# Moving the next input's normalisation into the second cross attention, in a two-block decoder kernel on one Trainium2 core

## What is computed

```python
x = x + L0_attn(layernorm(x))        # one head; scores from shell features
x = x + L0_xattn(layernorm(x), ctx)  # 8 heads over 64 context rows
x = x + L0_ffn(layernorm(x))         # one of 8 experts, chosen per batch
x = x + L1_attn(layernorm(x))        # 16 heads, causal
x = x + L1_xattn(layernorm(x), ctx)  # 16 heads over 64 context rows
x = x + L1_ffn(layernorm(x))         # gated, quantised weights and activations

def L0_attn(x):
    q = tanh(x @ W_charge.T + b_charge)
    shell = normalise(x @ W_shell.T + b_shell)
    proj = shell @ omega.T + rff_bias
    phi = outer(powers(q), concat(cos(proj), sin(proj))) @ W_combine.T
    attn = softmax(causal(phi @ phi.T * decay / temp))
    return (attn @ (x @ W_v.T + b_v)) @ W_out.T + b_out
```

## Time and profile before

| | us |
|---|---|
| median of 3 runs | 3010.41 (3004.92 to 3012.23) |
| the profiled execution | 3010.78 |
| its span, first to last instruction | 3008.8 |
| granted TensorE clock, mean | 0.867 |

### The profile page before, as it was taken

One profiled execution on the slowest core, in us unless ns is written; L12 is line 12 of the kernel. 1 busy time (PEld: TensorE's weight loads), 2 busy tenths in 40 slices (PEclk: granted clock), 3 DMA queues, 4 the chain that ended last, 5 costly groups with the idle time before them and its releaser, 6 DMA issues.

```text
span 3008.8 us, 50636 instructions
## 1 busy us (share of the span) xinstructions
PE 2276.8 (76%) x17470; PEld 1830.6 (61%) x17470; DVE 2175.1 (72%) x4246; ACT 1060.2 (35%) x2004; POOL 585.9 (19%) x666
## 2 busy tenths in 40 slices
PE   3667788868776877886877687888677777888875
PEld 3556666657465756664755565666565566666663
DVE  6765788866866578885776667888586666788767
ACT  2312444422432244442242224444224223444324
POOL 2111222212101122221101112222120102222220
PEclk8778899989777889998877789999877878999988
DMA  6001689840001078983000119897100014899600
GB/s 234 1 15 40 137 160 171 154 86 1 1 15 56 15 149 161 170 152 63 1 1 15 56 37 167 166 164 144 31 1 15 1 55 85 161 169 166 113 1 14
DMA packets 658407, 251.39 MB, mean 84 GB/s; under 512 B 613082, under 2 KB 633946, under 8 KB 657370
## 3 DMA queue, kind: packets, MB, share of 16 engines
q1 hardware_dynamic: 653978, 243.79, 41.4%
q10 hardware_dynamic: 4160, 4.19, 0.4%
HBM read 52.87 MB, written 10.49 MB: 21 GB/s over the span
## 4 chain that ended last, share of the span: by engine, by line
issue 38%; PE 23%; DVE 18%; DMA 11%; ACT 5%; POOL 4%; DVEq 1%; ACTq 0%; SPq 0%; POOLq 0%
DMA l_ptb<-l_phb 6%; PE ps L233 5%; PE ps L235 5%; PE ps L234 4%; DMA l_pts<-l_phs 4%; DVE nmax L1385 3%; PE ps L1289 1%; DVE l_k L1440 1%; DVE l_q L1444 1%; DVE l_phb L1391 1%; DVE l_phs L1391 1%; ACT l_q L1351 1%; PE ps L1271 1%; ACT xn L1347 1%; POOL d_pn L990 1%
## 5 line engine op out<-in xcount | busy, mean ns | idle before, releaser
L1385 DVE TENSOR_REDUCE nmax<-ps 128x1 f32<-128x1024 f32 (+7 forms) x512 | 383.3, 750 | 23.0 <-PE ps L1273 20.9
L1494 POOL CAST l_phb<-l_pb 128x1024 f16<-128x1024 f32 (+3 forms) x256 | 241.4, 943 | 654.1 <-ACT l_pb L1336 337.8
L1336 ACT ACTIVATE l_pb<-ps,nmax 128x1024 f32<-128x1024 f32 (+3 forms) x256 | 244.7, 956 | 283.5 <-DVE nmax L1385 282.7
L1271 PE MATMUL ps<-l_k,l_q 128*128 128x512 f32 (+3 forms) x768 | 319.1, 416 | 24.3 <-ACT l_ps L1336 23.9
L1391 DVE TENSOR_TENSOR l_phb<-l_pb,l_phb 128x1024 f16<-128x1024 f32 (+3 forms) x256 | 288.2, 1126 | 15.5 <-POOL l_phb L1494 13.4
L1272 PE MATMUL ps<-l_k,l_q 128*128 128x512 f32 (+3 forms) x768 | 270.1, 363 | 0.0
L1289 PE MATMUL ps<-l_v,l_ptb 128*128 128x64 f16 x4992 | 197.8, 197 | 34.2 <-DMA l_ptb<-l_phb 34.1
L1289 PEld LDWEIGHTS ps<-l_v,l_ptb 128*128 128x128 f16 x4992 | 177.1, 101 | 67.4 <-DMA l_ptb<-l_phb 41.1
L233 PE MATMUL ps<-xTh,l_w 128*128 128x512 f32 x256 | 123.1, 481 | 83.9 <-DVE l_q L1444 50.5
L1494 POOL CAST l_phs<-l_ps 128x128 f16<-128x128 f32 (+3 forms) x256 | 124.2, 485 | 319.1 <-DMA l_pts<-l_phs 169.6
L1271 PEld LDWEIGHTS ps<-l_k,l_q 128*128 128x128 f32 x768 | 156.0, 203 | 44.2 <-ACT l_ps L1336 29.8
(11 more groups left out here) (361 smaller groups left out, 6279.4 us busy)
## 6 DMA issues: line engine op xcount, KB each, us to landing
l_k<-xn SPq DMA_DIRECT2D x128, 256.0 KB, 4.1
l_w<-l_wqk_s SPq DMA_DIRECT2D x32, 512.0 KB, 4.8
l_wv<-l_wv_s SPq DMA_DIRECT2D x16, 512.0 KB, 6.0
xin<-in_x SPq DMA_DIRECT2D x4, 1024.0 KB, 5.5
m_w<-in_m_w SPq DMA_DIRECT2D x8, 512.0 KB, 4.4
m_w<-in_m_w SPq DMA_DIRECT2D x4, 1024.0 KB, 9.2
l_wo<-in_l_wo SPq DMA_DIRECT2D x16, 256.0 KB, 4.5
l_ptb<-l_phb SPq DMA_TRANSPOSE x256, 4.1
```

What stands on the lines that cost most here:

```text
L1271: pe.matmul(s[:, c0:c1], q, L["l_k1"][:, h, c0:c1], start=True, stop=False)
L1336: s.activation(l_numer(k)[:, 0:n], l_banks(k)[:, 0:n], ACT.Exp, bias=nmax[:, k % 4:k % 4 + 1], accum_out=lsum[:, h, k % NT:k % NT + 1]).th ...
L1385: v.tensor_reduce(nmax[:, k % 4:k % 4 + 1], l_banks(k)[:, 0:n], AX.X, ALU.max, negate=True).then_inc(q_["max"], 1)
L1494: g.tensor_copy(l_parts(k)[:, 0:cols], l_numer(k)[:, 0:cols]).then_inc(q_["hi"], 1)
```

## The change

- The first normalisation leaves the chain. `f_v_norm` has seven steps: 0 to 3 take statistics of two tiles each, 4 aggregates them and makes the reciprocal roots, 5 and 6 write four scaled tiles each. In D with a next batch, steps 0 to 4 stand ahead of `soft(0)` and steps 5 and 6 behind `sum_(1)`. They wait for the load of `xin`. The results lie in arrays of their own (`n_*`), in memory that D leaves free and that G's `g_h` and later arrays take over.
- At the head of G, PE transposes the four groups into four banks (4 to 7): two behind `turn_x(0)`, one behind `turn_x(1)`, one behind `updown(1)`. ACT copies two ahead of `silu(0)`, one ahead of and one behind `silu(1)`. DVE's residuals stand two ahead of `hidden(0)` and two behind it.
- All later steps of the chain come two values of t sooner on every engine. The combinations of four tiles and the two last value groups move ahead of `down(6)`, and DVE's second combination ahead of `add(7)`. The combination products use two banks in turn, where they had six.
- `f_pe_value` ends each value tile with one matmul of a row of ones with `bvo`; POOL's addition to `xin` and the wait for it are gone.
- The opening pass runs the same steps, the normalisation in one piece.

Cut to its core:

```diff
+        def f_v_norm(v, b, k, w):
+            if k < 4:
+                if k == 0:
+                    v.wait_ge(s_xin, b * 16 + 16)
+                for t in (2 * k, 2 * k + 1):
+                    v.bn_stats(w["n_st"][:, t, :], xin[:, t, :])
+            elif k == 4:
+                v.drain()
+                for t in range(NT):
+                    v.bn_aggr(w["n_ag"][:, t, :], w["n_st"][:, t, :])
+                v.drain()
+                v.tensor_scalar(w["n_nv"][:], w["n_ag"][:, :, 1], EPS, None, ALU.add)
+                rsqrt(v, w["n_rsd"][:], w["n_nv"][:])
+            else:
+                for t in range(4 * (k - 5), 4 * (k - 5) + 4):
+                    v.tensor_scalar(w["n_xn"][:, t, :], xin[:, t, :], w["n_ag"][:, t, 0:1], w["n_rsd"][:, t:t + 1],
+                                    ALU.subtract, ALU.mult).then_inc(s_x0, 1)
+        def f_pe_turn(pe, b, g, w):
+            pe.wait_ge(s_x0, b * NT + 4 * (g // 2) + 4)
+            for c in range(DC):
+                for t in range(2):
+                    o = ps[:, f_bank(g), c * 256 + t * P:c * 256 + (t + 1) * P]
+                    last = pe.transpose(o, w["n_xn"][:, 2 * g + t, c * P:(c + 1) * P], idf[:])
+            last.then_inc(s_tr, 1)
...
         def f_pe(pe, b, t):
-            if t in (0, 1):
-                ln_pe(pe, b, 0, (2 * t, 2 * t + 1))
-            elif t == 2:
+            if t == 0:
                 pe.wait_ge(s_lo, ln_done(b, 0))
...
+            elif t in (4, 5):
+                for u in (2 * t - 8, 2 * t - 7):
+                    pe.wait_ge(a_sem["ph"], b * 2 + 1)
+                    if u < 2:
+                        pe.wait_ge(a_sem["va"], b * 4 + u + 1)
+                    else:
+                        pe.wait_ge(a_sem["ya"], b * NT + u - 1)
+                    f_pe_comb(pe, u)
             elif t == 6:
                 pe.wait_ge(C0.s["kvT"], b * 2 + 2)
...
+                pe.wait_ge(a_sem["ph"], b * 2 + 2)
+                for u in range(4, NT):
+                    if u < 6:
+                        pe.wait_ge(a_sem["ya"], b * NT + u - 1)
                     f_pe_comb(pe, u)
                 for g in (2, 3):
-                    pe.wait_ge(a_sem["ya"], b * NT + g + 1)
                     f_pe_value(pe, b, g)
+            elif t == 7:
                 x_pe_m(pe, C0, b)
...
         def comb_bank(u):
-            return (0, 1, 2, 3, 6, 7, 0, 1)[u]
+            return (6, 7, 6, 7, 6, 7, 0, 1)[u]
...
                 for c in range(DC):
-                    last = mm3(pe, o, xTh[:, c, tok], xTl[:, c, tok], wvo_h[:, c, :], wvo_l[:, c, :], c == 0, c == DC - 1)
+                    mm3(pe, o, xTh[:, c, tok], xTl[:, c, tok], wvo_h[:, c, :], wvo_l[:, c, :], c == 0, False)
+                last = pe.matmul(o, ones_f[0:1, :], bvo[0:1, :], start=False, stop=True)
             last.then_inc(a_sem["v"], 1)
...
         def f_g(g, b):
             x_diagonal_first(g, b)
-            g.wait_ge(s_xn, b * (NPH * NT) + NT)
-            g.tensor_tensor(xin[:], xin[:], bvo[:].unsqueeze(1).to_broadcast([P, NT, D]), ALU.add).then_inc(s_xb, 1)
...
         def x_v(v, cr, b, more=False):
...
+            if more:
+                for k in range(5):
+                    f_v_norm(v, b + 1, k, N)
             soft(0)
             soft(1)
             sum_(0)
             sum_(1)
+            if more:
+                for k in (5, 6):
+                    f_v_norm(v, b + 1, k, N)
...
             turn_x(0)
+            if more:
+                f_pe_turn(pe, b + 1, 0, N)
+                f_pe_turn(pe, b + 1, 1, N)
             pe.wait_ge(g_sem["xT"], b * 2 + 1)
...
             turn_x(1)
+            if more:
+                f_pe_turn(pe, b + 1, 2, N)
             updown(1)
             pe.wait_ge(g_sem["xT"], b * 2 + 2)
+            if more:
+                f_pe_turn(pe, b + 1, 3, N)
+                pe.wait_ge(s_lo, b * (NTR * NG) + NTR * NG + 2)
```

More of the change, by code:

```diff
@@ L219, in decoder_kernel @@
         s_xn = sem("s_xn")
+        s_x0 = sem("s_x0")
+        LNT = (NPH - 1) * NT
         s_tr = sem("s_tr")
@@ L265, in ln_step @@
             order = ln_order(n)
[L266 to L271, removed]
+            size = NT // 2
+            v.wait_ge(s_xu, b * (NPH * NT) + (n - 1) * NT + k + 1)
             v.bn_stats(st[:, order[k], :], src[:, order[k], :])
@@ L285, in ln_step, with f_bank, f_turned, f_a_upper @@
                                 ALU.subtract, ALU.mult).then_inc(s_xn, 1)
-        def ln_v(v, b, n, src):
-            for k in range(NT):
-                ln_step(v, b, n, src, k)
+        N0 = {"n_xn": xn, "n_st": st, "n_ag": ag, "n_nv": nv, "n_rsd": rsd}
+        def f_v_norm(v, b, k, w):
[15 more added lines that the diff above has]
+                                    ALU.subtract, ALU.mult).then_inc(s_x0, 1)
+        def f_bank(g):
+            return 4 + g
+        def f_pe_turn(pe, b, g, w):
[5 more added lines that the diff above has]
+            last.then_inc(s_tr, 1)
+        def f_turned(g):
+            return ps[:, f_bank(g), :].rearrange("p (c t) -> p c t", c=DC), slice(2 * g * P, (2 * g + 2) * P)
+        def f_a_upper(s, b, g):
+            bank, cols = f_turned(g)
+            s.wait_ge(s_tr, b * (NTR * NG) + g + 1)
+            s.copy(xTh[:, :, cols], bank).then_inc(s_hi, 1)
+        def f_v_lower(v, b, g):
+            bank, cols = f_turned(g)
+            v.wait_ge(s_hi, b * (NTR * NG) + g + 1)
+            v.tensor_tensor(xTl[:, :, cols], bank, f32(xTh[:, :, cols]), ALU.subtract).then_inc(s_lo, 1)
         NTR = NPH - 1
@@ L608, in f_a @@
                     f_a_value(s, b, g)
+            elif t in (5, 6):
+                for u in (2 * t - 10, 2 * t - 9):
+                    f_a_comb(s, b, u)
             elif t == 7:
[L610 to L613, removed]
+                for u in range(4, NT):
                     f_a_comb(s, b, u)
@@ L616, in f_a @@
                     f_a_value(s, b, g)
+            elif t == 8:
                 x_a_m(s, C0, b)
@@ L633, in f_v @@
         def f_v(v, b, t):
[L635 to L639, removed]
+            if t == 1:
                 for g in range(2):
@@ L654, in f_v @@
                 last.then_inc(a_sem["shn"], 1)
[L655 removed]
+            elif t == 2:
                 for g in range(2):
@@ L685, in f_v @@
                 x_v_bias(v, C0, b)
-            else:
+            elif t == 7:
                 f_v_comb(v, b, 1)
+            elif t == 8:
                 x_v_m(v, C0, b)
@@ L933, in x_a, with x_v @@
                     exp(t + 2)
-        def x_v(v, cr, b):
+        def x_v(v, cr, b, more=False):
             q = cr.s
@@ L974, in x_v @@
                 if t == 0:
-                    v.wait_ge(s_xb, b * 4 + (2 if cr is C0 else 4))
+                    v.wait_ge(s_xb, b * 3 + (1 if cr is C0 else 3))
                 else:
@@ L1659, in g_v @@
             if more:
-                f_v(v, b + 1, 0)
+                for g in range(2):
+                    f_v_lower(v, b + 1, g)
             hidden(0)
+            if more:
+                for g in range(2, NG):
+                    f_v_lower(v, b + 1, g)
             for t in range(NT):
@@ L1691, in g_a @@
             copy_x(0)
+            if more:
+                for g in range(2):
+                    f_a_upper(s, b + 1, g)
             silu(0)
             copy_x(1)
+            if more:
+                f_a_upper(s, b + 1, 2)
             silu(1)
+            if more:
+                f_a_upper(s, b + 1, 3)
             for t in range(NT):
@@ L1935, in v_rest @@
             ln_lo(v, b, 4)
-            x_v(v, C1, b)
+            x_v(v, C1, b, more)
             g_v(v, b, more)
@@ L1996, in _ @@
             s.wait_ge(s_sv, SV)
+            for g in range(NG):
+                f_a_upper(s, 0, g)
             for t in range(NT + 1):
-                if t == 6:
+                if t == 4:
                     s.wait_ge(s_ws, 64)
@@ L2011, in _ @@
             setup_split_v(v)
+            for k in range(7):
+                f_v_norm(v, 0, k, N0)
+            for g in range(NG):
+                f_v_lower(v, 0, g)
             for t in range(NT + 1):
@@ L2025, in _ @@
             x_pe_kv(pe, C0, 0)
+            for g in range(NG):
+                f_pe_turn(pe, 0, g, N0)
             for t in range(NT + 1):
```

43 lines of the change are left out of this document (17 added, 26 removed).

## The result

The changed kernel takes 3046.35 us (median of 4 runs, 3043.74 to 3058.83), the kernel before 3011.32 us (4 runs, 3004.92 to 3018.29). The ratio is 1.0113, with a 95% interval of 1.009 to 1.0137: slower by 1.1%, where 3001 us and a range of 2985 to 3012 were forecast. The profiled execution took 3046.56 us (span 3044.8), 36.0 us of span more than before.

A forecast was written before the change was run, and what follows sets the result against it. No engine alone bounds: D is PE's stage, in G DVE's list nearly fills the stage. G -4.1 and D +2.1 make -2.0 a round, -6.0 over three; opening -3.1; 3010.8 becomes 3001.7, said as 3001 us; range 2985 to 3012.

The forecast's parts named there:

- D: Second cross attention, up to the first instruction of `g_v`; PE's stage, forecast 2.1 us longer a round from the moved scalings.
- G: Last feed-forward of a batch, with the next batch's opening attention steps woven in; forecast 4.1 us shorter a round.
- The opening pass: Opening pass: `a_k` keeps its 0.42 us, -4.1, against 1.0 for bias and alternating banks; -3.1 us together.
- The value bias: Value products: eight one-row bias products a batch at 0.226 us each, doubled at low clock; 1.8 to 3.6 us of PE.
- The tail of G: DVE's wait for `down(6)`, behind 5.4 us of combination, value and bias products at the high clock; 2.8 us.
- a term of 1.0: Opening pass: bias of the first two value groups plus combinations alternating between two banks; 1.0 us, bounds 0 and 3.
- low clock through the rest of G: Rival: value and tail products of the last feed-forward run at low clock, +9.0 us a round; 3029 us, chance 0.07.
- the bound of 2.1: Second cross attention: the eight scalings start only when POOL is done, delaying `d_tl` by 2.1 us; the upper bound, taken.
- The wait for the shell products: Last feed-forward: DVE waits 9.3 us for `down(0)` behind 48 shell products priced at the low clock, where it was 5.92.
- The head: Start of the last feed-forward: DVE waits 2.4 us for `silu(0)` and 0.6 for the last residual before `hidden(1)`.
- the middle: Last feed-forward: small DVE waits behind `om` and behind the value products; 2.7 us where it was 0.40.
- Behind `down(7)`: End of the last feed-forward: DVE waits of 3.1 and 2.1 us remain, for 2.26 and 2.30 before.

## Why the prediction was wrong

**The value bias: the step that failed.** It said eight products a batch at 0.226 each, "at the low clock twice that: 1.8 to 3.6 us of PE a batch". Three things are wrong in it. The row that it used, 16 plain fp32 products in 3.62 us, counts records, and such a product is two records, as those of the bias are (64 for 32): 0.45, not 0.226, and that is what 128 rows measured, 0.44. Then it is a row of products of 128 rows among their like. A product of one row between products of 128 takes 0.82 at the high level and 1.44 at the low one, 6.6 to 11.5 us a batch; the upper end of the bound was too low by a factor of three. And it held the level of the rest fixed, where the level came back much later.

A nearer row by shape was in the trace of before. The first cross attention ends each score with a one-row product, its mask; timeline of PE and of the weight loads there:

```profile
179.48 0.40 PE L235 MATMUL ps<-c_mh,xTl 128*128 128x512 f32 x1
179.81 0.38 PE L879 MATMUL ps<-mrow,ones_b 1*128 1x512 bf16 x1
180.12 0.66 PE L887 MATMUL ps<-idf,c_pn 128*128 128x128 f32 x4
```

```profile
179.80 0.09 PEld L879 LDWEIGHTS ps<-mrow,ones_b 1*128 1x128 bf16 x1 [0.36 <-issue]
180.12 0.42 PEld L887 LDWEIGHTS ps<-idf,c_pn 128*128 128x128 f32 x4 [0.23 <-issue]
```

The products before it start 0.23 apart; it starts 0.33 behind the last of them, its weights are not loaded ahead, and the loading stands still for 0.23 us behind it. That is the pause on both sides that the bias products show, seen on the only line of one-row products that the kernel had. The second cross attention adds its bias with a product of 128 rows, and there it stands among its neighbours without a pause:

```profile
681.53 0.40 PE L877 MATMUL ps<-e_b,ones_k 128*128 128x512 f32 x1
681.77 0.40 PE L233 MATMUL ps<-d_mh,xTh 128*128 128x512 f32 x1
```

Its neighbours start 0.23 apart, and so does the product behind it (0.24). So both forms of a bias, the dear and the cheap, lay side by side in the trace of before.

**The tail of G.** `down(6)` was priced behind 5.4 us of products at the high level, and the wait at 2.8. It is 10.69: the second value group takes 9.83 us and more for what was put at 24 x 0.11 + 4 x 0.226 = 3.5, and what follows starts at the low level. With the bias off TensorE the same wait is 2.57 and 3.99 us, so the term was right but for the bias.

**The opening pass.** The -4.1 for `a_k` was right (0.42 at 89.66, and the pass without any bias takes 116.8, 2.5 less than before, for a forecast of 3.1 less). The bias there shared a term of 1.0, with bounds of 0 and 3, with the alternating banks; it is 13.6 by itself, and the rest of the term comes to 4.1 - 2.5 = 1.6.

**The rival "low clock through the rest of G"**, 3029 us with a chance of 0.07, named what went along with the loss, but as something that might happen, without a cause in the change. It would have made G 9.0 - 4.1 = 4.9 us longer than before; measured are 7.7, 1.4 and 9.4. The second value group of the changed kernel's second round ran at the high level (5.54 us for 9.83), and that G took 101.2, 6 to 7 us less than the other two. 4.3 of these are the group's own; that the level is behind the rest too is likely, not shown. The rival was right in kind. Its weight was wrong, since nobody had asked what the bias products do to the level.

**D: right.** The statistics wait 0.45 us for the load and `soft(1)` takes it up. The eight scalings take 4.66 us beside POOL's `d_pn` for 2.67, but they are not all put off until POOL is done, as the bound of 2.1 had it: the first takes 0.81 us, the second 1.99, until 0.15 after POOL's last, and the other six their 0.40 each. The first `d_tl` comes 1.4 us later against the head of D (19.47 for 18.05). D is 2.3, 1.7 and 1.4 us longer for a forecast of 2.1, and moving the scalings away takes it back. The Trainium skill (SBUF — State Buffer, section "Who interferes with whom") has the rule that foresees it, whichever of DVE and GpSimd comes first blocks the other; the 4.66 us here and the 4.08 of `g_inv` agree.

**G without the bias: right in sign, too small.** -4.1 a round was forecast, after 0.9 for the bias; with no bias G is 6.7, 5.3 and 5.7 us shorter. The wait for the shell products was forecast at 9.3 (775.4 + 10.3 + 1.7 - 778.3 makes 9.1) and is 8.96 (9.13 without bias). The head was put at 3.0 us of waiting and is 0.7 (0.56), the middle at 2.7 and is 0.8 without bias: there the forecast was too dear. Behind `down(7)` it was too cheap: 3.1 and 2.1 were put down, and 4.93 and 1.43 are measured without bias.

**The sum.** 3001 us was said for the moves and a cheap bias. The moves alone, or with a bias of 128 rows, give 0.995 and 0.9956 of the kernel before: 2996 and 2998 us on its 3011. So the forecast came within 3 to 5 us of the time that the change would have had without its one-row products, with G's gain put some 5 us too small; the 49 us of the one-row products are the error.

## What to carry to other kernels

Price a new product by a row in which the number of rows changes as it will at the new place, not only by width and type, and count its records before dividing. A bias that already stands on all partitions goes into PSUM with weights of 1/128 over 128 rows; here that took 0.44 us a tile and the one-row form 0.82 to 1.44, with a lower granted clock around it. And a step that moves DVE work in between other work has to be laid beside POOL's list, not only into a gap of DVE: two of this change's scalings were held until POOL's instructions had ended, and POOL's own addition, once it came earlier, held an instruction of DVE for 4 us.

## What the runs showed of the hardware that was not expected

- A bias product of 64, 32 or 1 rows between products of 128 rows costs the same: 1.52 us for a tile at the high level and 2.72 at the low one, where 128 rows take 1.14 at the high one. Its weights are not loaded beside the product ahead, and the loading pauses behind it. It is the change in the number of rows that shows this, 0.19 us each time at the high level: products of 64 rows in a row are loaded ahead like those of 128. The Trainium skill (TensorE: Matmul & The Clock Gate, section "LDWEIGHTS (loading the stationary operand)") says that a weight load of 32 rows takes as long as one of 128. The loads themselves bear it out, 0.29 us with one row and 0.31 with 128; the cost is in what they no longer overlap. The same page (section "Step-by-step: what each phase is for") says that a load is pulled ahead of a running product where the row groups don't conflict or it goes to the background buffer; that a load with another number of rows than the product ahead is not pulled ahead here is what the rows show; why is left open.
- Such products go along with a longer low granted level though PE's records cover the stretch without a gap: 0.50 in 816.7 to 830.2 with 13.50 us busy of 13.50, and in 845 to 855 with 10.00 of 10. With 64 rows 6 of 8 value groups lie at a mean level below 0.6, with 128 rows none. They do not bring the level down each time: the changed kernel's second group of the second round, begun at 1589.85, ran its 5.54 us at 1.00. Whether it is the pauses or the missing rows themselves that the level follows stays open: no run had the one without the other.
